# A fused decoder block with routed experts on one NeuronCore: where VectorE does its spare work, and in which order the last groups run

## What is computed

```
x = x + attn(ln(x))     # q, k = relu(..) + 1e-6; num = q . cumsum(k v); den = max(q . cumsum(k), 1e-6)
                        # 16 heads of 16; out = (num / den) @ out_w.T + out_b
x = x + xattn(ln(x))    # one head against 77 context rows, softmax, output projection
x = x + ffn(ln(x))      # shared: ln(silu(x1) * x2) @ w3 + b3 for every token;
                        # 512 chosen tokens are also routed to the best of 8 experts,
                        # weights = softmax([shared score, best expert score])
                        # chosen tokens: shared_w * shared_out + expert_w * expert_out
```

## Time and profile before

| | us |
|---|---|
| median of 3 runs | 391.17 (390.69 to 391.75) |
| the profiled execution | 390.68 |
| its span, first to last instruction | 388.7 |
| PE busy | 364.0 (94%) |
| DVE busy | 300.7 (77%) |
| POOL busy | 278.8 (72%) |
| ACT busy | 164.8 (42%) |

### The profile page before, as it was taken

One profiled execution on the slowest core, in us unless ns is written; L12 is line 12 of the kernel. 1 busy time (PEld: TensorE's weight loads), 2 busy tenths in 40 slices (PEclk: granted clock), 3 DMA queues, 4 the chain that ended last, 5 costly groups with the idle time before them and its releaser, 6 DMA issues. The chain is left out here.

```text
span 388.7 us, 10585 instructions
## 1 busy us (share of the span) xinstructions
PE 364.0 (94%) x3489; PEld 262.7 (68%) x3489; DVE 300.7 (77%) x934; ACT 164.8 (42%) x395; POOL 278.8 (72%) x417
## 2 busy tenths in 40 slices
PE   8999999999999999999999999999899999997971
PEld 3475677777677777767767766777676666756751
DVE  2656888988889889798889888888565567799771
ACT  3172444454355345435535532534356445423320
POOL 5135978777677776677776687878978888586475
PEclk9999999999999999999999999999999999999997
DMA  7993592300210120031412003003000233134720
GB/s 232 336 277 81 150 316 85 83 15 15 49 37 26 25 63 17 16 70 35 158 37 47 16 19 80 15 16 81 17 29 14 80 99 108 56 123 158 232 98 16
DMA packets 38077, 33.32 MB, mean 86 GB/s; under 512 B 4426, under 2 KB 37225, under 8 KB 38025
## 3 DMA queue, kind: packets, MB, share of 16 engines
q1 hardware_dynamic: 35432, 28.68, 25.7%
q0 software_dynamic: 1456, 3.37, 3.0%
q10 hardware_dynamic: 1136, 0.60, 0.7%
HBM read 15.58 MB, written 13.78 MB: 76 GB/s over the span
## 5 line engine op out<-in xcount | busy, mean ns | idle before, releaser
L1545 POOL TENSOR_TENSOR s_t<-s_t,causal 128x512 f32<-128x512 f32 x63 | 79.9, 1288 | 16.2 <-ACT s_t L881 16.2
L500 PE MATMUL bank<-h1t,w_qkv 128*128 128x512 f32 x112 | 53.2, 597 | 2.6 <-DVE x L1128 2.6
L1115 DVE TENSOR_TENSOR s_t<-sbank,causal 128x512 f32<-128x512 f32 x65 | 43.6, 674 | 1.3 <-PE sbank L521 1.0
L1537 POOL TENSOR_TENSOR state_wide<-state,own_pair 128x256 f32<-128x256 f32 x28 | 17.2, 614 | 31.0 <-DVE state L1106 29.3
L881 ACT ACTIVATE s_t<-sbank 128x512 f32<-128x512 f32 x63 | 33.8, 588 | 7.8 <-PE sbank L521 7.7
L521 PE MATMUL sbank<-arena 32*128 32x256 f32 x512 | 36.7, 400 | 0.0
L560 PE MATMUL bank<-s_t,vp 128*32 128x128 f32 x1024 | 34.6, 275 | 2.0 <-POOL s_t L1545 1.1
L638 PE MATMUL bank<-w_out,attn_t 128*128 128x256 f32 x128 | 34.4, 391 | 0.9 <-DVE attn_t L1195 0.7
L507 PE MATMUL bank<-w_qkv,h1t 128*128 128x256 f32 x128 | 34.1, 389 | 0.0
L1553 POOL TENSOR_TENSOR rr<-ve,neg_half 128x3 f32<-128x3 f32 x36 | 32.0, 888 | 3.0
L731 PE MATMUL sbank<-h1t,w 128*128 128x512 f32 x72 | 33.2, 597 | 0.5 <-ACT h1t L881 0.5
(11 more groups left out here) (215 smaller groups left out, 831.5 us busy)
## 6 DMA issues: line engine op xcount, KB each, us to landing
rden_t<-rden SPq DMA_DIRECT2D x64, 64.0 KB
rows<-x SPq DMA_DIRECT2D x32, 128.0 KB, 1.7
x<-in_x SPq DMA_DIRECT2D x7, 512.0 KB, 7.5
out<-x SPq DMA_DIRECT2D x7, 512.0 KB
we<-in_we SPq DMA_DIRECT2D x1, 2048.0 KB
rows<-empty SPq DMA_DIRECT2D x1, 1419.0 KB, 6.8
rows<-empty SPq DMA_DIRECT2D x1, 1408.0 KB, 7.1
xmask<-in_mask POOLq DMA_DIRECT2D x2, 616.0 KB, 6.5
```

Source lines behind the costliest of these rows:

```text
L500: mm = pe.matmul(dst[:, :], w_qkv[:, ch, cb * P:(cb + 1) * P], h1t[:, g % 3, ch, :], start=(ch == 0), stop=(ch == CH - 1))
L1115: dve.tensor_tensor(s_t[:, r, :, :], sbank[r][:, :].rearrange("p (s q) -> p s q", s=4), causal[:, :].unsqueeze(1).to_broadcast([P, 4, P]), ...
L1545: pool.tensor_tensor(s_t[:, r, :, :], s_t[:, r, :, :], causal[:, :].unsqueeze(1).to_broadcast([P, 4, P]), ALU.mult)\
```

## The change

1. DVE runs the four bias parts after the loop, at the head of its iterations q = 3, 4, 5 and 6, no longer in steps 16, 20, 24 and 28.
2. In DVE's steps with `i % 4 == 3` the second `by_queries` stands behind L1195, the state update and `rsum`. The first stays where it was. (L1195 holds the scaled numerators, so that the scaling stands between the two products.)
3. ACT takes the exponential of `pair_d` one iteration later, after the gates of q = 8. POOL waits for `pair_ready` before `bias_tiles(7)`.
4. PE, in q = 8: output products of unit 7 ahead of the transposes of M0.
5. PE, in q = 10 and 11: `z_features(q - 1)` between the two halves of the gate products instead of behind the second (q = 9 had it so before). DVE, in q = 10: `normalize_blocks(9)` ahead of `y_evict(8)`.

```diff
@@ PE
-                    if half == (0 if q == FIRST_M else 1):
+                    if half == (0 if FIRST_M <= q < NU else 1):
                         z_features(pe, q - 1)
-                to_features(pe, q + 1)
+
+                if q != FIRST_M - 1:
+                    to_features(pe, q + 1)
                 if q == GATHERED:
                     route_ranks(pe)
                 y_products(pe, q - 1, expert, load_expert if q == FIRST_M - 1 else None)
+                if q == FIRST_M - 1:
+                    to_features(pe, q + 1)
@@ ACT
             for q in range(3, NU + 1):
                 gates(q, 0)
                 gates(q, 1)
+                if q == GATHERED + 2:
+                    act.wait_ge(pair_ready, 1)
+                    act.activation(pair_e[:, :, :], pair_d[:, :, :], ACT.Exp).then_inc(pair_exp, 1)
...
-                if q == GATHERED + 1:
-                    act.wait_ge(pair_ready, 1)
-                    act.activation(pair_e[:, :, :], pair_d[:, :, :], ACT.Exp).then_inc(pair_exp, 1)
@@ DVE, step
                     if i % GT == 3:
-                        for ch in range(CH):
-                            by_queries(g, ch)
+                        by_queries(g, 0)
...
                     dve.reciprocal(rsum[:, B % 2:B % 2 + 1], psum_[:, B % 2:B % 2 + 1]).then_inc(rsum_done, 1)
+
+                if g < NG and i % GT == 3:
+                    by_queries(g, 1)
...
-                if i % GT == 0 and 16 <= i < 32:
-                    split_biases((i - 16) // GT)
@@ DVE, behind the loop
             for q in range(3, NU + 2):
+                if 3 <= q < 7:
+                    split_biases(q - 3)
                 if q == GATHERED - 2:
                     gathered_stats()
+                if q == FIRST_M + 1:
+                    normalize_blocks(q - 1)
                 y_evict(q - 2, 0, GT if q != NU else 2)
...
-                normalize_blocks(q - 1)
+                if q != FIRST_M + 1:
+                    normalize_blocks(q - 1)
@@ POOL
                 elif q == GATHERED + 1:
                     invert_variance(q - 1)
+
+                    pool.wait_ge(pair_ready, 1)
                     bias_tiles(q)
```

## The result

The changed kernel took **386.18 us** (median of 4 runs, 386.08 to 386.28) beside 391.46 us for the kernel before (4 runs, 390.69 to 392.54): ratio 0.9869, 95% interval 0.9843 to 0.9895, so faster by 1.3%. The forecast was 387.6 us, in a range from 385.5 to 390.3, with a chance of 0.84 for faster. The profiled execution took 386.19 us with a span of 384.2 (before: 390.68 and 388.7), 4.5 less, where the sum had said 3.6. In the largest set of runs the kernel before fell into two groups, 390.07 to 390.69 us (9 of 19 executions, mean granted clock 0.994 to 0.996) and 391.77 to 392.66 us (10, clock 0.989 to 0.992), so a median moves with the mix, and of the 5.3 us between the two medians above the 4.5 of the spans is the safer figure.

A forecast was written before the change was run, and what follows sets the result against it. PE bounds the kernel, busy 364.0 us, 94% of the span, so time is its work plus few waits. Terms -2.3 - 2.0 + 1.1 - 0.4 = -3.6 took 391.17 to 387.6 us, range 385.5 to 390.3.

The forecast's parts named there:

- Parts out of the loop: Steps 16, 20 and 24: without the bias parts PE's three L500 waits for x1 go, -2.3 us (bounds -2.6 and 0).
- Second product behind attn_t: Seven loop steps (3, 7, ... 27): PE's projection L638 waits less for DVE's attn_t, -2.0 us, lower bound -2.6.
- The drawing of step 19: Loop step 19: attn_t starts 0.6 us earlier, second product runs 188.8 to 189.45, L1115 ends 190.1, L638 ends 189.96.
- The deduction towards x1: Seven loop steps: x1 and projection meet within 0.1 us, just room; -2.0 taken where waits and restarts would be 2.6.
- third rival: Loop: second product loses to POOL's state_wide, waits 0.61 us, x1 late; +4.3 over seven steps, 393.9 us; chance 0.06.
- Parts behind the loop: q = 3 to 5: parts delay POOL through shared ports, and PE's wait for the read; three times 0.34, +1.1 us.
- Rival 2: Behind the loop: parts hold POOL for their whole time, +3.3 in place of +1.1, 389.8 us; chance 0.12.
- rival 1: Behind the loop: parts cost nothing there, and the tail gives its bound; -5.6, 385.6 us; chance 0.13.
- Weights: Behind the loop: pair_d loses some 2.1 us less, DVE keeps about 1.2; by itself nothing of it reaches PE.
- Products ahead of M0's transposes: PE, q = 8: unit 7's products fill the read wait, but ACT's eviction is then uncovered; only -0.4 us arrives.
- take 1.75 and fit into the 2.21: PE, q = 8: unit 7's products last 1.75 us and fit into the 2.21 us wait for the sorted tokens' read.
- z_features between the halves: PE, behind the loop: transposes 1.0 us earlier, second half's gates 0.4 later, products after evict_z no earlier; cost 0.

## Why the prediction was right, and where it was off

*Parts out of the loop, -2.3: right in kind, 2.78 measured.* The forecast took the waits of L500 and their restarts (2.57) and then took 0.3 off because PE can catch up. It did not catch up: the steps got shorter by 0.91, 0.75 and 1.12, a little more than the waits say. The mis-sized step is that deduction.

*Second product behind attn_t, -2.0: right, 2.47 measured,* close to the lower bound of 2.6. The drawing of step 19 held to 0.1 us, and POOL gave way as expected (1.05; "about 1.2" was said). The deduction towards x1 was again too careful: with 1.07 us from L638 to x1, PE never waits for it in these steps. The third rival fell, but both products behind `attn_t` showed that its mechanism is real and cost 3.14 us of the loop there, all of it in the four of the seven steps that have a state update, 0.6 to 0.9 us each. The change keeps clear of it with a lead of 0.09 us. The rival counted its 0.61 in seven steps; POOL's `state_wide` follows the product in four.

*Parts behind the loop, +1.1: 1.07 measured* at M0. The sign and the path were right (POOL late, then `y_evict`), but that the size fits is partly luck: the forecast priced three transfers longer by 0.34 each, and the two that got longer did so by 0.08 and 0.16. Counted from the loop's end, `y_evict` starts later than before by 0.33 at q = 3, by 0.24 at q = 4 and by 1.09 at q = 5. Part 0 lengthened two of POOL's gathers (1.20 and 1.14 in place of 1.12 and 0.98), which makes `z_r` 0.22 later. Part 1 ran beside a `z_r` that took 1.22 in place of 1.05, and left POOL some 0.5 behind, which nobody at q = 4 felt. Part 2 ran beside the normalization of the gathered tokens, 1.53 in place of 1.10, and was itself held up (L1344 took 0.67, and 0.42 where it was alone); with both, POOL was 0.94 behind, and `y_evict` waits for POOL's `z_r`. (Just ahead, L1645 was 0.46 longer and L1647 0.51 shorter than before, which nearly cancels.) The normalization and part 2 in the changed kernel:

```profile
318.25 1.53 POOL L1651 TENSOR_SCALAR arena<-arena,g_nm,g_rstd 128x256 f32<-128x256 f32 x2
319.38 0.67 DVE L1344 CAST be<-be_rest 8x512 bf16<-8x512 f32 x1
```

The normalization in the kernel before:

```profile
323.09 1.10 POOL L1642 TENSOR_SCALAR arena<-arena,g_nm,g_rstd 128x256 f32<-128x256 f32 x2
```

The two gathers in the changed kernel, POOL:

```profile
303.42 1.20 POOL L1639 DMA_INDIRECT arena<-rows,idx_u  x1 [0.17 <-issue]
304.92 1.14 POOL L1639 DMA_INDIRECT arena<-rows,idx_u  x1 [0.31 <-issue]
```

The cast L1337 (304.10, 0.39 long) ran beside the first and the two-input L1338 (304.52, 0.69) beside the second. The gathers have these lengths within 0.01 in all eight profiles with the parts behind the loop, and 1.12 and 0.97 or 0.98 in the six without. So a cast beside a gather now has a row, which the forecast missed. The Trainium skill, "SBUF — State Buffer", in its paragraph "DVE blocks DMA", says that GpSimd cannot write the descriptors of its transfers while VectorE runs a 2-port operation. The sign agrees, but the gather beside the cast lengthened by 0.08 only, and the one beside L1338, which is no such operation, by 0.16. Whether the cast ran in such a mode no row says.

Rival 2, +3.3, fell; so did rival 1, which had the parts free. It took the runs with the parts moved to tell: the time of 386.2 by itself is nearer to rival 1's 385.6 than to the 387.6 of the forecast.

*Weights.* The forecast had `pair_d` short because POOL now starts its addition behind it. It is short (0.17), but the new wait has no part in it here, as the run without it showed; the parts behind the loop shift POOL against DVE enough. With the parts elsewhere the wait does hold POOL.

*Products ahead of M0's transposes, -0.4: 0.06 to 0.15 measured* (the run with the old order, and the way to M0 without parts, 67.00 against 67.15). That the stall only changes its name was right, with 1.27 us for the 1.4 forecast. The step that failed is "take 1.75 and fit into the 2.21": they took 2.46. The weight loads of these products have three gaps of 1.4 us in all, with "issue" as the cause. The code has two `load_expert`, register loads, between these products. Behind the queued transposes (the run with the old order) the same products with the same loads took 1.92. That the loads make the gaps once nothing is queued ahead is argued from this and was not tried apart.

*z_features between the halves, 0: a loss of 0.5 measured* where nothing is late (26.95 against 26.43, one profile of the old order), and 0.35 between the two first profiles. The step that failed is that a tanh 0.5 later moves nothing behind it: it moved `evict_z` and the products by 0.3. Where ACT's copies are late the new order did better, so its worth over all executions is open.

*Not in the sum:* M0 to M1 got shorter by 0.41. In the profiled execution of the kernel before, ACT's copies for M1 were 0.97 late, and in that of after 0.04. As the kernel with late parts shows, this comes and goes between sets of runs of one kernel, so it is no gain of the change. The interval of the ratio (4.1 to 6.1 us) is wide enough for it.

The sum of what was measured: -2.78 - 2.47 + 1.07 - 0.15 + 0.35 - 0.41 = -4.39, and -0.09 at the start, against -4.5 for the spans. The forecast of -3.6 missed a gain of 0.95 in the loop and the unforeseen 0.41, and it missed losses of 0.25 for the order of the products and 0.35 for z; that these partly cancel is luck. The further 0.8 to the medians' difference of 5.3 is the before side: its profiled execution was 0.8 under its median in that set.

## What to carry to other kernels

Where the busiest engine has 94% and the rest are its waits for one other engine, read each wait together with what stands ahead of the awaited instruction on that engine, and move only as much behind it as the next deadline allows; here one product fitted in every step, and two only in the steps without a state update on DVE and POOL. Small work is best put where its engine already waits for the bounding one (the last steps of the loop: 0.9 to 1.1 us better than the stretch behind it, which is a chain through all engines). A transfer's wait that vanishes from PE's list is no gain until the next wait on the same path is subtracted: of 2.2 us the start of M0 moved by about 0.1.

## What the runs showed of the hardware

A two-input DVE operation on 8 numbers per partition took 0.16 or 0.17 us where no POOL operation held it, and 0.53, 1.20 or 2.31 beside POOL's additions and multiplications on whole tiles, ending each time with the POOL operation that had started just before it; its size says nothing of its cost there. In contrast POOL's tiny operation z_r (342.52, 1.04 long) left DVE's operations of 0.16 to 0.19 beside it at their usual length, two-input ones among them (`pair_d`, 343.29, 0.17).

ACT's copies for M1 began 0.03 to 0.04 us behind PE's transposes in five profiles and 0.7 to 1.2 behind in nine, while ACT was idle and nothing in the records explains the delay. In six of the nine the tanh ahead of the copies was late too, by 0.4 to 0.9 us behind PE's L746 where it is 0.04 in all others, so the delay is not one of the copies alone. In four of those nine, all with the z order of before, PE also waited 0.2 to 0.5 before a group of L744 with "issue" as the cause. It went by sets of runs: in each set of experiments all profiles had it or none had. The first profiles of before (late) and after (on time) differ in it. On the way from M0 to M1 it cost 0.5 and 0.9 us in the two kernels seen both ways (7.71 against 7.23, and 7.95 against 7.05). What it is stays open; no kernel here could take it away.
